# Context attention's keys, values and first queries moved into the delta rule's last steps, into its spent buffers

## What is computed

```python
def step(S, inp):
    q_t, k_t, v_t, b_t = inp
    pred = jnp.einsum('bhk,bhkv->bhv', k_t, S)
    S = S + b_t[..., None, None] * (k_t[..., None] * (v_t - pred)[..., None, :])
    o_t = jnp.einsum('bhk,bhkv->bhv', q_t, S)
    return (S, o_t)
...
x = _layernorm(x + _L0_attn_ref(x, L0_attn_Wq, ...), axis=-1)
```

```python
q = (x @ Wq).reshape(B, S, H, D).transpose(0, 2, 1, 3)
k = (c @ Wk).reshape(B, N, D, H).transpose(0, 3, 2, 1)
v = (c @ Wv).reshape(B, N, D, H).transpose(0, 3, 1, 2)
mask = jnp.all(c == 0, axis=-1)[:, None, None, :]
scores = jnp.einsum('bhsd,bhdn->bhsn', q, k) * scale
...
return out @ Wo
```

## Time and profile before

| | us |
|---|---|
| median of 3 runs (lowest, highest) | 2899.11 (2895.47, 2906.67) |
| the profiled execution | 2897.46 |
| its span in the trace | 2895.7 |
| PE busy | 2574.3 (89%) |
| VectorE busy | 2235.2 (77%) |
| ScalarE busy | 1411.6 (49%) |
| GpSimd busy | 506.2 (17%) |

### The profile page before, as it was taken

How to read it: one execution, slowest core, us unless ns; L and a number is a source line. 1 busy time by engine, 2 the same in 40 slices (tenths; PEclk the granted TensorE clock), 3 DMA queues, 4 the chain that set the end, 5 groups by cost and what they waited for, 6 DMA issues and landing times. The chain is left out here.

```text
span 2895.7 us, 83026 instructions
## 1 busy us (share of the span) xinstructions
PE 2574.3 (89%) x35314; PEld 1816.0 (63%) x35336; DVE 2235.2 (77%) x4040; ACT 1411.6 (49%) x2549; POOL 506.2 (17%) x661
## 2 busy tenths in 40 slices
PE   7798888898987768999999987897779999998998
PEld 5666666666665537766776664443367777765665
DVE  3898998889998516888888884987768888870886
ACT  7667657765675102333333223544356666641454
POOL 2233322332233100000000000004501111110122
PEclk9899999999997679999999998998989999998999
DMA  2000111110101040122211113538951212213332
GB/s 86 21 15 33 55 40 33 33 55 33 40 33 40 33 190 15 51 67 71 61 59 52 59 59 126 180 113 279 325 160 44 88 59 78 69 62 106 120 114 79
DMA packets 172717, 234.24 MB, mean 81 GB/s; under 512 B 17858, under 2 KB 94018, under 8 KB 171332
## 3 DMA queue, kind: packets, MB, share of 16 engines
q1 hardware_dynamic: 172356, 229.01, 23.9%
HBM read 136.18 MB, written 92.80 MB: 79 GB/s over the span
## 5 line engine op out<-in xcount | busy, mean ns | idle before, releaser
L722 ACT ACTIVATE delta_product<-delta_line,delta_conv_w 128x256 f32<-128x256 f32 x576 | 248.6, 496 | 7.1 <-DVE delta_conv L892 5.9
L1285 PE MATMUL ctxatt_banks<-ctxatt_xT,ctxatt_wq 128*128 128x256 f32 x1024 | 232.4, 380 | 2.9 <-ACT ctxatt_qT L1361 2.1
L1324 PE MATMUL ctxatt_banks<-ctxatt_wo,ctxatt_oT 128*128 128x512 f32 x512 | 229.4, 601 | 4.9 <-DVE ctxatt_norm_y L1436 4.9
L1285 PEld LDWEIGHTS ctxatt_banks<-ctxatt_xT,ctxatt_wq 128*128 128x128 f32 x1024 | 189.6, 190 | 28.5 <-ACT ctxatt_qT L1361 3.3
L949 DVE TENSOR_TENSOR delta_squares<-delta_t_sys 128x30 f32<-128x30 f32 (+14 forms) x480 | 178.1, 371 | 12.5 <-issue 0.2
L952 DVE TENSOR_TENSOR delta_t_sys<-delta_t_sys,delta_squares 128x30 f32<-128x30 f32 (+14 forms) x480 | 163.4, 341 | 16.5
L704 ACT ACTIVATE delta_line<-delta_banks,delta_proj_b 128x256 f32<-128x256 f32 x192 | 88.0, 458 | 173.5 <-PE delta_banks L533 173.4
L1324 PEld LDWEIGHTS ctxatt_banks<-ctxatt_wo,ctxatt_oT 128*128 128x128 f32 x512 | 95.8, 192 | 116.1 <-issue 109.6
L1371 ACT ACTIVATE ctxatt_probsT<-ctxatt_banks 128x512 f32<-128x512 f32 x128 | 69.4, 594 | 190.1 <-PE ctxatt_banks L1306 190.1
L596 PE MATMUL delta_banks<-delta_woT,delta_oT 128*128 128x512 f32 x256 | 133.0, 668 | 27.7 <-DVE delta_norm_y L1011 22.9
L1361 ACT ACTIVATE ctxatt_qT<-ctxatt_banks 128x512 f32<-128x512 f32 x64 | 38.2, 597 | 228.2 <-PE ctxatt_banks L1285 228.2
(11 more groups left out here) (356 smaller groups left out, 6287.6 us busy)
## 6 DMA issues: line engine op xcount, KB each, us to landing
h<-ffn_hid SPq DMA_DIRECT2D x66, 256.0 KB, 2.0
ffn_hid<-h SPq DMA_DIRECT2D x6, 1536.0 KB
delta_xT<-xT SPq DMA_DIRECT2D x16, 512.0 KB, 4.7
delta_x<-x SPq DMA_DIRECT2D x16, 512.0 KB, 3.6
xT<-delta_newT SPq DMA_DIRECT2D x16, 512.0 KB, 2.8
x<-delta_new SPq DMA_DIRECT2D x16, 512.0 KB, 4.0
ctxatt_xT<-xT SPq DMA_DIRECT2D x16, 512.0 KB, 4.8
ctxatt_x<-x SPq DMA_DIRECT2D x16, 512.0 KB, 4.9
```

Of the source, the lines that this page charges most:

```text
L722: made = act.activation(slot(n, i)[:, j - 1, g].rearrange("p (b t) -> p b t", b=B), line[:, i, g, :, j:j + P], ACT.Copy, scale=conv_w[:, i ...
L1285: mm = pe.matmul(b_q[:, i * B * P:(i + 1) * B * P], wq[:, k, pair * P:(pair + 1) * P], xT_sb[:, n.parity, k], start=k == 0, stop=k == KB - 1)
L1324: mm = pe.matmul(b_o[:], oT[:, b, k, :], wo[:, k, :], start=k == 0, stop=k == PAIRS - 1)
```

## The change

An object `ContextStart` allocates the tiles that both sublayers use: the delta rule's projection weights, columns, products, lines, convolutions and beta weights, with views for context attention's weights, keys, values, queries, mask and columns in the same memory. Each is filled when the delta rule has read it for the last time. Context attention's start is taken out of its function and written into the delta rule's lists, in its banks for projections:

- SyncE: `wv` and `cT` are loaded in step 16, once all projections are made; `wk` in step 17 behind `load_rows` of tile 14, once the convolutions are joined; `wq` once the four values are made; then the first two tiles of the delta rule's result.
- PE: four values, eight keys and the first job of queries stand in step 17, the second job of queries in step 18, the third and the count of filled numbers in step 19 ahead of the output projection of tile 15, the fourth ahead of its transposition.
- ScalarE keeps what PE makes (VectorE did). VectorE marks the filled numbers in step 17 and makes the mask at the end. GpSimd writes the ones.
- `context_attention` begins its loop with step 0 without work; `wo` is loaded at its start.

```diff
@@ delta_rule_attention, SyncE @@
+                def load_values():
+                    sp.wait_ge(projected, len(GROUPS) * STEPS)
+                    sp.dma_start(both.wv, both.w["wv"].rearrange("(k p) n -> p k n", p=P)).then_inc(wv_here, 16)
+                    sp.dma_start(both.cT, both.ctxT.rearrange("(k p) b n -> p k b n", p=P)).then_inc(wv_here, 16)
+
+                def load_keys():
+                    for i in range(3):
+                        sp.wait_ge(joined[i], JOIN_OPS * STEPS)
+                    sp.dma_start(both.wk, both.w["wk"].rearrange("(k p) n -> p k n", p=P)).then_inc(wk_here, 16)
+
+                def load_queries():
+                    sp.wait_ge(next_made, VALUES)
+                    sp.dma_start(both.wq, both.w["wq"].rearrange("(k p) n -> p k n", p=P)).then_inc(wq_here, 16)
...
+                    for i in range(2):
+                        sp.dma_start(both.xT[i].rearrange("p k n -> p (k n)"), xT_out_view[i:i + 1].rearrange("s p n -> (s p) n")).then_inc(first_here, 16)
@@ delta_rule_attention, PE @@
+                def next_bank(j):
+                    if j < 2:
+                        pe.wait_ge(lined, len(GROUPS) * STEPS)
+                        pe.wait_ge(beta_done, 2 * STEPS)
+                    else:
+                        pe.wait_ge(next_kept, j - 1)
+                    return b_proj[:, j % 2]
+
+                def values(j):
+                    bank = next_bank(j)
+                    if j == 0:
+                        pe.wait_ge(wv_here, 32)
+                    for k in range(KB):
+                        mm = pe.matmul(bank, both.cT[:, k, j // 2, :], both.wv[:, k, (j % 2) * 512:(j % 2 + 1) * 512], start=k == 0, stop=k == KB - 1)
+                    mm.then_inc(next_made, 1)
+
+                def keys(i):
+                    bank = next_bank(VALUES + i)
+                    if i == 0:
+                        pe.wait_ge(wk_here, 16)
+                    for k in range(KB):
+                        mm = pe.matmul(bank[:, 0:B * CTX], both.wk[:, k, i * P:(i + 1) * P], both.cT[:, k].rearrange("p b n -> p (b n)"), start=k == 0, stop=k == KB - 1)
+                    mm.then_inc(next_made, 1)
+
+                def first_queries(j):
+                    bank = next_bank(VALUES + KEYS + j)
+                    if j == 0:
+                        pe.wait_ge(wq_here, 16)
+                        pe.wait_ge(first_here, 32)
+                    for i in range(2):
+                        for k in range(KB):
+                            pair = 2 * j + i
+                            mm = pe.matmul(bank[:, i * B * P:(i + 1) * B * P], both.wq[:, k, pair * P:(pair + 1) * P], both.xT[0][:, k], start=k == 0, stop=k == KB - 1)
+                    mm.then_inc(next_made, 1)
...
@@ context_attention, PE @@
-                        if n:
+                        if n and n.index:
                             queries(n, u)
...
-                keys_and_values()
+                pe.sem_inc(projected, PAIRS // 2)
                 unrolled(pe, STEPS, LAG, step)
```

More of the change, by code:

```diff
@@ L609, in step, with count_filled @@
+                def count_filled():
+                    pe.wait_ge(masked, MASK_OPS * STEPS)
+                    pe.wait_ge(ones_made, 1)
+                    pe.wait_ge(filled_made, 1)
+                    for k in range(KB):
+                        mm = pe.matmul(b_kk[:, 0, 0:B * CTX], both.ones, both.filled[:, k], start=k == 0, stop=k == KB - 1)
+                    mm.then_inc(counted, 1)
                 def step(n):
                     t1, t2, t3, t4 = n.back(1), n.back(2), n.back(3), n.back(4)
+                    draining, ending, last = n.index == STEPS + 1, n.index == STEPS + 2, n.index == STEPS + 3
@@ L640, in step @@
                         project(t1, 12)
+                    if draining:
+                        keys(0)
                     if t3:
                         update(t3, 3)
+                    if last:
+                        first_queries(3)
                     if t4:
@@ L656, in step @@
                         project(n, 2)
+                    if draining:
+                        keys(3)
+                        keys(4)
                     if t1:
```

215 lines of the change are left out of this document (142 added, 73 removed).

## The result

| | before | after |
|---|---|---|
| median (lowest, highest), us | 2898.34 (2895.47, 2906.67), 4 runs | 2871.99 (2861.56, 2874.48), 4 runs |
| profiled execution, us | 2897.46 | 2872.21 |
| its span, us | 2895.7 | 2870.4 |
| PE busy, us | 2574.3 | 2562.2 |
| VectorE busy, us | 2235.2 | 2227.8 |

The ratio is 0.9893, 95% interval 0.9877 to 0.9909: faster by more than 0.5%. The forecast was 2867 us.

A forecast was written before the change was run, and what follows sets the result against it. Between sublayers a serial PE chain binds; in the drain VectorE, then a ring of short instructions. Saving 57.7 us, less 24 (drain) and 3 (cold start), takes 2897.5 to 2867 us; own range 2855 to 2879, final range 2850 to 2882.

The forecast's parts named there:

- Step 1: Step 17, values 0 ahead of `predict`: costs 6.4 us at the low clock, making VectorE's `miss` 4.8 us late.
- step 2: Values 1 to 3 at full clock in step 17: `add` comes 5.6 us late, `carry` 6.5 late.
- Step 3: Keys 0 to 2 in step 17: PE waits 5.5 us for `wk`, restarts cold, and `carry` comes 12.5 us late.
- Step 4: Keys 3 to 7 and queries 0 around tile 15's first `predict`: its first `update` comes 23.5 us late.
- Step 5: Up to `predict` of tile 15's third chunk, six warmer PE pieces give back 2 us: 21.5 late.
- Step 6: Step 18, queries 1 ahead of tile 15's outputs: net 2.5 us more, giving 24 late.
- Step 7: Step 19, queries 2, the count and queries 3: net +0.5 us, so the drain ends 24 us late.
- Step 8: Context attention starts with cold scores and queries after PE idles 5 us: +3 us, between 0 and 5.
- the drain hides nearly all: Rival, chance 0.15: dense work holds the clock up, the drain grows by only 10 us, total 2852 us.
- PE's instruction stalls grow: Rival, chance 0.10: loads in flight delay PE's instructions in the drain, another 10 to 12 us lost, total 2878 us.
- The two slower cases: Clock stays low through the drain, 2921 us, chance 0.04; or jobs push the drain out 50 us, 2893, chance 0.05.

The follow-up runs named there:

- the warm ones: Changed kernel with keys' load and SyncE's counts earlier, and queries late or four unread matmuls ahead of the barrier: third unit 12.42 us behind the barrier.
- the repeat: The changed kernel itself, traced and timed again against the kernel before: median 2865.17 us, ratio 0.9878.
- run 2: PE makes values 0 behind `predict` of tile 14's third chunk instead of ahead of it, against the changed kernel: drain 131.70 us.
- run 1: SyncE loads `wk` ahead of `load_rows` in step 17, against the changed kernel: drain 123.05 us, median 2871.25 us.
- run 3: Keys 3 to 7 and queries 0 compute only a quarter of their sums, against the changed kernel: drain 123.85 us, total 2862.08 us.
- run 6: SyncE raises its two counts for tiles already there ahead of context attention's loads, against the changed kernel: total 2869.02 us.
- run 4: Six matmuls that nobody reads put behind the delta rule's last transposition, against the changed kernel: total 2871.78 us.
- run 7's repeat: Second timing of the changed kernel with keys' load earlier, SyncE's counts first and queries 1 to 3 one place later: median 2859.85 us, ratio 0.9866.
- run 8: Changed kernel with keys' load earlier, counts first, queries 1 to 3 later, and also values 0 in step 16, values 1 to 3 earlier: total 2872.62 us.

## Why the prediction was right

The forecast was 30.7 us by a sum of three terms. Measured in the same terms: 57.7 us saved (57.74 from barrier to first scores before, 0.19 after, so 57.55), 24 given back in the drain (22.5), 3 in the loop's start (4.7, as the third unit came 17.14 behind the barrier against 12.42 in the warm ones): 30.3. The profiled execution is 5.4 us above the forecast because T0 and the rest took 2.2 and 2.8 more, which no step speaks of; the forecast lies between the two medians of the changed kernel, 2871.99 and 2865.17. That the sum came within 0.4 us is luck in part: a drain 1.5 us better and a start 1.7 us worse cancel.

| step, late against before | predicted | measured |
|---|---|---|
| 1: `miss` | 4.8 | 3.0 |
| 2: `add`; tile 14's third `carry` | 5.6; 6.5 | 4.4; 5.4 |
| 3: PE's wait for `wk`; the fourth `carry` | 5.5; 12.5 | 5.17; 10.9 |
| 4: tile 15's first `update` | 23.5 | 21.6 |
| 5: `predict` of its third chunk | 21.5 | 21.5 |
| 6: second half of step 18's projection | 24 | 24.7 |
| 7: last projection (24 + 3.5); the barrier | 27.5; 24 | 26.1; 22.5 |
| 8: cold start | 3 | 4.7 |

- **Step 1** priced values 0 at the lower clock, 6.4 us. It took 4.94 (938.67), 5.40 in the repeat: the clock rose within it. The lateness of `miss` was then taken as the start of a chain, and run 2 shows that it is not: with `miss` on time the drain was no shorter. The first wait that counts is VectorE's 5.31 us ahead of `add`, for PE, as in step 2.
- **Step 3** is right in cause, place and size: run 1 takes exactly this wait away by SyncE's order alone.
- **Step 4** is right: run 3 shows the jobs at nearly their full length. That `update` comes at 998.40, predicted 998.1, is partly luck, as T0 was 2.2 late and the jobs up to there 1.9 short.
- **Step 5** took the ring's pieces at 0.75 for 1.1 us; the rows at 998.40 and 1001.10 have 0.75 and 0.74. Two gaps on "issue" of 1.5 to 1.6 us came in and the clock fell again by 1010, so this step gave back 0.2 us and not 2. That its total is 21.5 as forecast is luck: the jobs ahead of it had cost 1.9 less.
- **Step 6** chose 2.5 between 1.7 and 4.5 and it was 3.2: queries 1 took 6.06 us at a rising clock, the projection behind took 3.70 for 5.59, and a gap of 1.5 us on "issue" ahead of them was not foreseen.
- **Step 7** priced queries 2 and the count cold, 8.3 us; they took 4.92 and 1.89 in this trace, 6.01 and 1.89 in the repeat, whose drain is 23.6 us late. Queries 3 was hidden as foreseen (3.62 us, with 1.39 of the wait ahead of the transposition left), and the warm projection and transpositions gave back 3.5 us, where 2.7 and 1 had been put down. (Its "net +0.5" should be 0.8 by its own terms, 3.5 less 2.7.) So the drain ended 1.5 us better than forecast.
- **Step 8** is the term that was mis-sized: 3 us, measured 4.7. The clock's part was right (2.8 by run 6); 1.9 us came from SyncE, which the forecast had not looked at. Its two counts for tiles that were already in SBUF stood behind the issues of six loads, each 0.4 to 0.7 us. The queries came 1.13 us later for it, and at a clock still lower: 6.32 us against 5.58 in run 6.

**The range.** If every piece ran warm and `wk` came without a wait, the forecast's own terms (3, 2 to 4, 2, 3 and 5) leave 7 to 9 of its 24 us, not the 9 to 11 that it gives. So the lower side of its own range reaches 15 to 17 us down and not 13 to 15, which the 2850 to 2882 that it ends with still covers.

**The rivals.** That the drain hides nearly all was partly so: the mean granted clock rose from 0.66 to 0.87 and PE's existing work got 15.9 us shorter, but the drain still grew by 22.5 and not 10. That PE's instruction stalls grow fell: L620 waited 9.2 us for "issue" in 10 pieces, the longest 1.6, against 12.7, 11 and 2.9, with the loads of `wk`, `wq` and two tiles in flight. Over all of PE's lines from T0 to the barrier it was 16.7 us before and 8.5 after. Most of the difference lies in step 17: the kernel before has five gaps of 0.78 to 2.92 us in the first 37 us of its drain, 8.9 us together, and the changed kernel, with the jobs between the small pieces, has none above 0.57 in its first 60 us. The forecast had looked for the opposite only. The queue carried as many bytes as before:

```profile
q8 instruction: 278, 4.55, 0.7%
```

These are 16.4 KB a packet, which agrees with the 16 KiB blocks that the Trainium skill names in "Runtime: NRT & Kernel Launch", Instruction fetch mechanics. The page also has the fetch as mostly hidden; if the gaps on "issue" are late blocks, which no run here settles, it is hidden only in part, since they are 8 to 17 us of some 108 to 132 in each drain. The two slower cases did not occur: the clock rose within the first job, and in the last two steps the jobs were exposed only in part.

## What to carry to other kernels

A stage's one-time start is worth moving into the drain of the stage before it, though the drain pays: here 57.6 us went, and 22.5 came back in the drain and 4.7 in the next loop's start. Look for what pays: a load issued in program order behind a wait that it does not need (5 us), a count behind issues of other loads (1.9 us), and a clock that has fallen by the next stage's first matmul (2.8 us); each was mended by moving one call, and the last by letting a real job be PE's last work ahead of the barrier. A dense job holds the clock up for what stands behind it, so moving it away from a critical place can lose what it wins.

## What the runs showed of the hardware that was not expected

- A dense piece in front of small ones shortens them: the 32x32 pieces of the ring took 1.08 us before and 0.74 to 0.75 behind the jobs. PE was busy 36.9 us more for 52.8 us of added jobs.
- The clock was down again when PE had been idle for 6.39 us (scores 2.08 us), and still up after 1.95, 1.99 and 2.94 us (1.16 us). In run 4 it was up after 1.34 us of idling (scores 1.16 us) and down again in the queries (5.41 us for 3.72) behind another 2.02 us.
- A count on SyncE comes only after the issues ahead of it: it held PE for 1.13 us and, when PE was ready sooner, for 2.02.
- T0 varied from 935.6 to 944.9 us between kernels that do the same work up to the first moved load, at 907 us in the changed kernel, and by 3.2 between two executions of one kernel. Tile 14's second `miss` varied more, from 925.95 in run 7's repeat to 938.43 in run 8. This is more than the experiments' single effects. It arises early: SyncE's second `load_rows` (L447) stands at 193.20 us in one trace of the changed kernel and at 195.58 in the other. The cause is open.
- The same job in the same place took 4.56 to 6.07 us from trace to trace (queries 2, behind a transposition of 1.08 to 1.09 us each time).
- The same drain code gave 130.25, 131.27 and 131.37 us in three executions, and with `wk` early 123.05 and, up to its last microseconds the same, 125.79.
